# Gated RWKV and quantised FFN on one core: the residual stream stored early, and the FFN outputs added to it in HBM by accumulating DMAs

## The reference

```python
x = x + tanh(g_xattn) * rwkv(layernorm(x), ctx, ctx, w, u)
x = x + tanh(g_ffn)   * ffn(layernorm(x))
# ffn: xq = fake_quant(x); gate = xq @ Wg.T; up = xq @ Wu.T
#      h  = fake_quant(silu(gate) * up);  out = h @ Wd.T
```

## Time and profile before

| | us |
|---|---|
| median of 3 runs | 221.23 |
| lowest and highest run | 219.24 and 221.35 |
| the profiled execution, its own time | 221.53 |
| span of the profiled execution (first to last instruction) | 220.1 |
| busy in the span: PE, DVE, ACT, Pool | 172.1, 170.5, 156.0, 138.5 |
| DMA traffic: HBM read, written | 24.65 MB, 4.46 MB |

### The profile page before, as it was taken

One profiled execution on the slowest core, in us unless ns is written; L12 is line 12 of the kernel. 1 busy time (PEld: TensorE's weight loads), 2 busy tenths in 40 slices (PEclk: granted clock), 3 DMA queues, 4 the chain that ended last, 5 costly groups with the idle time before them and its releaser, 6 DMA issues.

```text
span 220.1 us, 3345 instructions
## 1 busy us (share of the span) xinstructions
PE 172.1 (78%) x1098; PEld 124.4 (57%) x1098; DVE 170.5 (77%) x344; ACT 156.0 (71%) x234; POOL 138.5 (63%) x157
## 2 busy tenths in 40 slices
PE   4499968989898999971076649959999943999960
PEld 4456528979898999960065533414343412776620
DVE  0769493648558689986699679496899998999992
ACT  3459698555995996987489965747998953899400
POOL 3455223559699799865788609984577670029991
PEclk9969996999999999998566755997999995599996
DMA  3999999999998995200000000000000000004468
GB/s 102 328 374 348 348 314 291 271 294 298 291 317 204 279 248 159 83 0 1 0 0 0 0 0 3 1 0 0 0 3 0 0 1 0 0 3 141 149 201 275
DMA packets 43328, 29.31 MB, mean 133 GB/s; under 512 B 2224, under 2 KB 43056, under 8 KB 43312
## 3 DMA queue, kind: packets, MB, share of 16 engines
q1 hardware_dynamic: 43168, 28.84, 45.8%
q10 hardware_dynamic: 144, 0.26, 0.3%
HBM read 24.65 MB, written 4.46 MB: 132 GB/s over the span
## 4 chain that ended last, share of the span: by engine, by line
PE 43%; ACT 14%; DVE 12%; DMA 9%; POOL 7%; issue 7%; SPq 6%; DVEq 1%; POOLq 0%; ACTq 0%
PE ps L1011 12%; PE ps L978 11%; PE ps L882 7%; PE ps L898 7%; DMA hidden<-lag_w 6%; PE ps L922 4%; DMA hidden<-in_ctx 3%; ACT hidden L499 3%; ACT z_t L506 2%; SPq L271 2%; PE ps L929 2%; ACT hidden L570 2%; POOL z_t L433 2%; DVE h_peaks L817 1%; SPq L278 1%
## 5 line engine op out<-in xcount | busy, mean ns | idle before, releaser
L898 PE MATMUL ps<-hidden 128*128 128x128 f32 (+1 forms) x512 | 60.5, 280 | 5.6 <-DVE hidden L645 2.5
L898 PEld LDWEIGHTS ps<-hidden 128*128 128x128 f32 x512 | 59.5, 196 | 7.1 <-issue 3.3
L397 POOL TENSOR_TENSOR x_all<-x_all,silu_out 128x512 f32<-128x512 f32 x16 | 24.4, 1537 | 8.1 <-DVE silu_out L707 8.0
L817 DVE TENSOR_REDUCE h_peaks<-hidden (+2 forms) x24 | 26.0, 1123 | 3.6 <-POOL hidden L441 3.2
L698 DVE SCALAR_TENSOR_TENSOR h_space<-z_t,ps 128x256 f32<-128x256 f32 x32 | 19.1, 600 | 10.9 <-PE ps L898 10.8
L1011 PE MATMUL ps<-wdT,z_t 128*128 128x256 bf16 (+1 forms) x192 | 26.0, 293 | 1.9 <-ACT z_t L629 1.9
L922 PE MATMUL ps<-ident,hidden 128*128 128x128 f32 x64 | 13.1, 374 | 15.9 <-POOL hidden L421 11.4
L629 ACT ACTIVATE z_t<-h_space 128x1024 bf16<-128x1024 int8 (+3 forms) x12 | 20.1, 1754 | 6.8 <-DVE h_space L845 6.8
L1011 PEld LDWEIGHTS ps<-wdT,z_t 128*128 128x128 bf16 (+1 forms) x192 | 17.6, 104 | 10.3 <-issue 4.8
L615 ACT ACTIVATE silu_out<-ps,mix_scale 128x1024 f32<-128x1024 f32 (+1 forms) x18 | 18.4, 1020 | 5.5 <-PE ps L978 3.2
L922 PEld LDWEIGHTS ps<-ident,hidden 128*128 128x128 f32 x64 | 10.8, 197 | 18.0 <-ACT hidden L499 17.3
(11 more groups left out here) (101 smaller groups left out, 340.8 us busy)
## 6 DMA issues: line engine op xcount, KB each, us to landing
hidden<-lag_w SPq DMA_DIRECT2D x26, 512.0 KB, 7.3
x_all<-in_x SPq DMA_DIRECT2D x8, 512.0 KB, 8.8
hidden<-in_ctx SPq DMA_DIRECT2D x8, 512.0 KB, 9.0
out<-x_all SPq DMA_DIRECT2D x16, 256.0 KB, 2.3
xq<-in_L_ffn_w_down SPq DMA_DIRECT2D x1, 704.0 KB, 5.9
xq<-in_L_ffn_w_gate SPq DMA_DIRECT2D x1, 640.0 KB, 7.3
h_space<-in_L_ffn_w_up SPq DMA_DIRECT2D x1, 640.0 KB, 6.0
lag_w<-up_out ACTq DMA_DIRECT2D x1, 255.0 KB, 7.4
```

The lines of the kernel that those rows point to most:

```text
L397: nc.gpsimd.tensor_tensor(xs, xs, mixed[:, m % 2, :, :].rearrange("p c b -> p b c"), ALU.add).then_inc(s["x1_done"], 1)
L817: nc.vector.tensor_reduce(h_peaks[:, bass.ds(KA * b + k, 1)], hidden[:, bass.ds(b * HB + k * BT, cols)], AX.X, ALU.max, apply_absolute_val ...
L898: last = nc.tensor.matmul(ps[:, j % BANKS, c * 2 * SEQS:end * 2 * SEQS], lag_tile(j)[:, c, :], ekp[:, (j * CK + c) * 2 * SEQS:(j * CK + en ...
```

## The change

SP stores x1 to the output as soon as it is complete, in eight DMAs of 512 KB. Pool waits until these have landed, and then, for each n, once DVE's product is in its slot of `ffn`, issues a DMA of that slot to the output with `accum_op=ALU.add`: the DMA engines read the slot and the output's present value, and write the sum to the output. Pool's 12 sums, DVE's four sums and SP's 16 late stores are gone. A slot may be written again when the DMA of n - 8 has landed (semaphore `added[n % 8]`, 16 per DMA), in place of when Pool's sum of n - 8 is done. SP waits at its end for all 16.

```diff
-        dve_sums = [n for n in range(SUMS) if n >= SUMS - 8 and n % 4 >= 2]
-        pool_sums = [n for n in range(SUMS) if n not in dve_sums]
...
+        added = [sem(f"added{i}") for i in range(8)]
...
-            for n in range(SUMS):
-                if n in dve_sums:
-                    sp.wait_ge(s["dve_sum_done"], dve_sums.index(n) + 1)
-                else:
-                    sp.wait_ge(s["sum_done"], pool_sums.index(n) + 1)
-                sp.dma_start(out_v[:, 2 * n:2 * n + 2, :], seqs(x_all, 2 * n, 2)).then_inc(s["out_done"], 16)
-            sp.wait_ge(s["out_done"], 16 * SUMS)
+            sp.wait_ge(s["x1_done"], PAIRS)
+            for g in range(GROUPS):
+                sp.dma_start(out_v[:, g * GS:(g + 1) * GS, :], seqs(x_all, g * GS, GS)).then_inc(s["x1_stored"], 16)
+            sp.wait_ge(s["x1_stored"], 16 * GROUPS)
+            for n in range(8):
+                sp.wait_ge(added[n], 16 * (SUMS // 8))
...
-            for n in pool_sums:
+            pool.wait_ge(s["x1_stored"], 16 * GROUPS)
+            for n in range(SUMS):
                 pool.wait_ge(s["ffn_done"], n + 1)
-                xs = x_all[:, n * 2 * C:(n + 1) * 2 * C]
-                nc.gpsimd.tensor_tensor(xs, xs, ffn[n // 4 % 2][:, n % 4, :], ALU.add).then_inc(s["sum_done"], 1)
+                pool.dma_start(out_v[:, 2 * n:2 * n + 2, :], ffn[n // 4 % 2][:, n % 4, :].rearrange("p (b c) -> p b c", c=C),
+                               accum_op=ALU.add).then_inc(added[n % 8], 16)
...
-                    wait(dve, s["sum_done"], n - 7)
+                    wait(dve, added[n % 8], 16 * (n // 8))
...
-                for n in [n for n in dve_sums if n // 4 == b]:
-                    dve.wait_ge(s["ffn_done"], n + 1)
-                    xs = x_all[:, n * 2 * C:(n + 1) * 2 * C]
-                    nc.vector.tensor_tensor(xs, xs, ffn[b % 2][:, n % 4, :], ALU.add).then_inc(s["dve_sum_done"], 1)
```

More of the change, by code:

```diff
@@ L225, in gated_rwkv_ffn @@
             "hpeak_done", "h_top_done", "h_topT", "row_ps",
-            "h8_done", "hq_done", "down_done", "ffn_done", "sum_done", "dve_sum_done", "out_done")}
+            "h8_done", "hq_done", "down_done", "ffn_done", "x1_stored")}
         x_in = [sem(f"x_in{g}") for g in range(GROUPS)]
         ring_in = [sem(f"ring_in{i}") for i in range(SLOTS)]
+        added = [sem(f"added{i}") for i in range(8)]
         weights_in = s["gate_in"], s["up_in"], s["down_in"]
```

## The result

The changed kernel takes 227.45 us, the median of five runs (226.05 to 231.84), against 221.23 for the kernel before: a ratio of 1.030, 95% interval 1.024 to 1.036. It is slower by 3.0%. The execution profiled there took 228.06 us with a span of 226.3.

The account below looks back on a forecast made before the run. It took TensorE's down products, then a 6.9 us tail, as the bound. Four pieces by 204.8, twelve at 1.51 us to 222.9, 1.1 us closing to 224.0, and 1.43 us above span gave 225.4 us; range 218.8 to 237.

Parts of the forecast that it names:

- The early stores at nothing: Eight x1 stores in the DMA engines' idle stretch, landed by about 119 us: no cost, up to 12.1 us without that cover.
- The transfer at 1.51 us a piece: Last stage: each 256 KB accumulating DMA takes 1.51 us of all 16 engines, bounds 0.76 and 1.51.
- a share of 1.02: DMA busy share during the late plain stores at 217 to 218 us, read as leaving no room for another read.
- a draw: Rival: issue or transfer takes 0.96 to 1.32 us, own time 219.3 to 223.7 us, within 1%; chance 0.20.
- Four pieces moved by 204.8: Start of the DMA stream: Pool's first four issues end at 203.3, the fourth transfer at 204.8 us.
- The issue on Pool at 1.0 us, hidden: Each Pool DMA issue takes 1.0 us, bounds 0.37 to 2.36, hidden behind a 1.51 us transfer except the first.
- Pool beside DVE's quantising: From 198.27 us, DVE quantising block 3 costs Pool's first four issues 2.64 us, bounds 0 and 3.36.
- The new waits hold nothing: DVE's product n waits for DMA n - 8 to land; binds only above about 1.8 us a piece, so costs nothing.
- Closing, 1.1 us from the last byte: End of the kernel: 1.1 us from the last DMA byte to the span's end, kept from the kernel before.
- the tail: Stretch behind DVE's last product, 213.18 to 220.1: 6.9 us, of which 2.9 sums, 0.9 issue, 2.4 landing, 0.7 closing.
- My two figures for the most that could be gained: At the kernel's end: a gain not over 3.8 us less a Pool issue, and the 217.6 us of the faster case.
- the faster rival: The second read hides at 0.76 us a piece, Pool issues well under 1 us, end follows last product: 217.6 us; chance 0.12.

Follow-up runs that it names:

- the second profile: The changed kernel unchanged, run and profiled once more against the kernel before: 227.96 us, ratio 1.032 (1.023 to 1.041).

## Why the prediction was right

The forecast was 225.4 us, slower, because the sum would go at the pace of accumulating transfers that read twice. The direction holds, and so does the pace as the cause: without the add in the DMA the time is 10 us or more lower, halving Pool's issues wins nothing, and the waits and the early stores cost nothing. That a transfer is slow because it reads twice is not shown: the page of the profile counts 24.65 MB read from HBM in both kernels, so the second read does not appear in the trace, and no run parts the read from the addition. Step by step, with the rows of the second profile:

- *The early stores at nothing.* Right: 104 to 118 us, and 1.002 when added alone.
- *The transfer at 1.51 us a piece.* Right in kind, too high: 1.34 us in the steady stretch. The 1.75-fold price of a plain piece, 1.34 to 0.76, is under the two that I took. My reason, that a share of 1.02 leaves no room for a second read, did not hold as stated: the share rose to 1.24, so the accumulating packets overlap more than the plain ones did. The rule of "Collectives: The Full Stack" in the Trainium skill that I had weighed, half the rate for two reads, agrees with 196 to 347 GB/s within that eighth. But the size matters: with 1.34 us my own sum gives 204.8 + 12 x 1.34 + 1.1 + 1.43 = 223.4 us, just inside what I had called a draw (up to 223.7). The rest of the 3% came from the start and the end of the stream, which I had not foreseen, so that the forecast lies within 1.2% of the profiled time is in part luck.
- *Four pieces moved by 204.8.* Too early by 2.6 us: at 108 and 141 GB/s the fourth is through at about 207.4. Of this, 0.8 is the later first issue (197.47 for 196.64, of which 0.25 are older than the stage). The other 1.8 are the slow start, whose cause is open; by the ends of its issues Pool was ahead.
- *The issue on Pool at 1.0 us, hidden.* Too small: 1.24 us each in the steady run, and 0.725 without the add. It was still hidden, by a margin of 8% and not of a third.
- *Pool beside DVE's quantising.* I charged 2.64 us to the first four issues. They took 6.16 us where each later four took 4.94, so 1.2 us were lost. With plain issues, four took 5.20 us in place of 4 x 0.725 = 2.9, so 2.3 us were lost there, beside two pieces of DVE of 3.28 us together. The rule from "SBUF — State Buffer" of the Trainium skill, by which all 3.28 would be lost, agrees in direction and not in size.
- *The new waits hold nothing.* Right for the end, wrong for the reason. I had them bind only above 1.8 us a piece. They bind for 4.7 us, and the last product comes 2.3 us later, because the slow start of the stream puts the landing of the eighth piece at 214.8 and not at 211.2. The run with 16 slots shows that the end does not care.
- *Closing, 1.1 us from the last byte.* Right: from about 225.0 to 226.3 are 1.3 us. But behind the first four pieces, twelve at 1.34 us would have been through at 223.5. The last bytes came 1.5 us later, as the rate was a little lower until 216 (186 and 190 GB/s) and the engines did not end together.

The forecast of 225.4 is 2.7 us under the 228.06 of that execution: 0.8 for the later first issue, 1.8 for the slow start, 2.0 back for the shorter steady pieces, 1.5 for the slightly lower rate and the uneven end, 0.2 for the closing and 0.3 between span and own time (1.76 for 1.43), with the rest in rounding.

What the tail had to give is seen where the DMAs keep up: with half of the rows the ratio is 0.994 (0.989 to 0.998), though that kernel leaves half of the outputs out. My two figures for the most that could be gained do not agree: 3.8 us less an issue of 0.37 is 3.4, while the faster rival at 217.6 is 3.9 under the profiled 221.53. The rival's sum took 1.9 us of landing behind the issue where SP had waited 2.4.

## What to carry to other kernels

Before sums are moved into accumulating DMAs, count the DMA engines' time: here a 256 KB piece took 1.34 us of all 16 of them at best in place of 0.76 for a plain store, so 16 pieces need 21 us and more, and a stage that makes them in 17 ends on the DMA. The early store of the residual was free and the relief of Pool and DVE was real, but the adds stood in the queue in front of the last bytes. A mixture does not escape that by itself: while accumulating transfers are queued, plain stores behind them wait too.

## What the runs showed of the hardware that I had not expected

- Pool's issue depends on the kind and not only on the size: 0.725 us for a plain store of 256 rows of 1 KB, 1.24 us in a steady run for the accumulating one of the same shape, and 1.27 us for an accumulating one of 512 rows. Why twice the rows are not dearer is open.
- Pool's plain stores put the 4.2 MB into 1280 packets, its accumulating ones into 4352, about one for each of the 4096 rows. Pool's plain packets thus carried several rows. SP's plain stores were 4352 packets too and wrote 347 GB/s, so the number of packets alone does not make the rate low.
- A busy DMA share of 1.0 to 1.2 says little about the bytes: it stood beside 108, 141 and 196 GB/s of accumulating transfers in one kernel, and beside 347 of plain stores in the other.
